# A perceiver layer on one core: the attention's value product in two passes per head, and weight sums in halves or later

## The reference, cut to what matters

```python
def _L0_xattn_ref(q, latent_kv, Wq, Wkv_expand, Wout):      # q: 512 x 1024; the mask leaves 512 keys
    qh, kh, vh = ...                                         # 16 heads of 64
    scores = where(causal, qh @ kh.T / 8, -inf)
    return concat(softmax(scores) @ vh) @ Wout.T

def _L0_attn_ref(x, w_gate, norm_gate, w_down, norm_down):   # w_gate 5632 x 1024, w_down 1024 x 2816
    def weight_quant(w):
        scale = 1.0 / clip(mean(abs(w)), 1e-5, None)
        return clip(round(w * scale), -1, 1) / scale
    gate, up = split(bitlinear(x, w_gate, norm_gate))        # bitlinear: rms norm, integers of x, w quantised
    return bitlinear(silu(gate) * up, w_down, norm_down)

x = x + _L0_xattn_ref(layernorm(x), ctx, ...)
x = x + _L0_attn_ref(layernorm(x), ...)
x = x + _L0_ffn_ref(layernorm(x), ...)                       # 8 experts, top 2, and a shared one
```

## Time and profile before

| | |
|---|---|
| time of three runs | 632.73 us median (631.98 to 633.84) |
| profiled execution | 634.08 us, its span 632.3 us, so 1.8 us lie around the span |
| TensorE | 612.3 us busy of 632.3, clock granted 0.997 |
| VectorE, ScalarE, GpSimd | 510.8, 422.5, 193.6 us busy |
| attention pairs | 34 to 147 us |
| output product | 147 to 200 us |
| gate product | 200 to 278 us |
| down product | 278 to 323 us |
| experts | 323 to 632 us |

### The profile page before, as it was taken

How to read it: one execution, slowest core, us unless ns; L and a number is a source line. 1 busy time by engine, 2 the same in 40 slices (tenths; PEclk the granted TensorE clock), 3 DMA queues, 4 the chain that set the end, 5 groups by cost and what they waited for, 6 DMA issues and landing times.

```text
span 632.3 us, 10608 instructions
## 1 busy us (share of the span) xinstructions
PE 612.3 (97%) x3624; PEld 478.2 (76%) x3625; DVE 510.8 (81%) x887; ACT 422.5 (67%) x558; POOL 193.6 (31%) x174
## 2 busy tenths in 40 slices
PE   8999999998999999999989999999999999999996
PEld 6778888887886444444557888898988989889775
DVE  5888888888787777889998569688796887969687
ACT  4998888889755989784575347557384673846630
POOL 2354446426000333527920220040431404214051
PEclk9999999999999999999989999999999999999999
DMA  8977776865246997936999467796876958779357
GB/s 333 418 294 300 304 303 238 314 262 193 101 167 265 404 374 294 384 122 251 393 368 397 195 245 280 252 369 226 318 283 240 365 222 332 262 261 354 129 171 271
DMA packets 31070, 177.91 MB, mean 281 GB/s; under 512 B 4064, under 2 KB 4064, under 8 KB 14784
## 3 DMA queue, kind: packets, MB, share of 16 engines
q1 hardware_dynamic: 25536, 158.64, 65.4%
q0 software_dynamic: 5504, 18.88, 8.2%
HBM read 154.30 MB, written 23.20 MB: 281 GB/s over the span
## 4 chain that ended last, share of the span: by engine, by line
PE 62%; DVE 15%; ACT 13%; issue 5%; DMA 3%; POOL 2%; DVEq 0%; POOLq 0%; SPq 0%; ACTq 0%
PE BK L2155 11%; PE BK L306 9%; PE BK L1884 8%; PE BK L2158 4%; ACT RA L1385 4%; ACT PR L1412 4%; PE BK L312 3%; PE BK L313 3%; PE BK L318 3%; PE BK L2125 3%; DVE WL L1033 2%; PE BK L2113 2%; PE BK L1829 2%; PE BK L2111 2%; DMA RX<-wbit 1%
## 5 line engine op out<-in xcount | busy, mean ns | idle before, releaser
L2155 PE MATMUL BK<-EX,WH 128*128 128x320 f32 x384 | 99.4, 342 | 0.0
L702 POOL TENSOR_TENSOR WL<-RC,WH 128x2048 fp32r<-128x2048 f32 x7 | 45.6, 6517 | 167.6 <-ACT WH L1588 167.6
L1033 DVE TENSOR_TENSOR WL<-RA,WH 128x2048 fp32r<-128x2048 f32 x40 | 89.4, 2287 | 9.0 <-ACT WH L1588 8.8
L2158 PE MATMUL BK<-EX,WL 128*128 128x160 f32 x336 | 79.3, 236 | 0.0
L1588 ACT ACTIVATE WH<-RA 128x2048 fp32r<-128x2048 f32 x40 | 73.6, 1904 | 0.3 <-PE BK L1927 0.2
L2155 PEld LDWEIGHTS BK<-EX,WH 128*128 128x128 f32 x384 | 69.2, 189 | 0.0
L2158 PEld LDWEIGHTS BK<-EX,WL 128*128 128x128 f32 x336 | 64.1, 191 | 0.0
L652 POOL TENSOR_TENSOR HB<-HB,ND (+2 forms) x26 | 28.7, 1122 | 100.3 <-DVE BH L919 99.7
L1484 ACT ACTIVATE RA<-RA,RT 128x2048 int16<-128x2048 f32 x22 | 43.8, 1999 | 3.0 <-DVE RT L849 2.0
L1693 ACT ACTIVATE HX<-SR 128x320 fp32r<-128x320 f32 x16 | 7.6, 472 | 57.0 <-DVE SR L1083 57.0
L1884 PE MATMUL BK<-TG,XQ 128*128 128x512 bf16 x192 | 42.4, 379 | 0.1
(11 more groups left out here) (331 smaller groups left out, 1672.6 us busy)
## 6 DMA issues: line engine op xcount, KB each, us to landing
RA<-wbit SPq DMA_DIRECT2D x54, 1024.0 KB, 6.4
RA<-wmoe SPq DMA_DIRECT2D x40, 1024.0 KB, 6.4
RC<-wmoe SPq DMA_DIRECT2D x20, 1024.0 KB, 7.9
rows<-ZERO POOLq DMA_DIRECT2D x40, 256.0 KB, 8.1
XG<-rows SPq DMA_DIRECT2D x10, 512.0 KB, 3.6
rows<-YS SPq DMA_DIRECT2D x9, 512.0 KB, 4.2
RA<-wqk SPq DMA_DIRECT2D x7, 640.0 KB, 8.1
RA<-wo SPq DMA_DIRECT2D x4, 1024.0 KB, 7.8
```

The lines of the kernel that those rows point to most:

```text
L702: e.tensor_tensor(WL[2][:, at], RC[5][:, :], WH[2][:, at].bitcast(f32), ALU.subtract).then_inc(free_c[5], 1)
L1033: e.tensor_tensor(WL[m][:, q * RAW:q * RAW + RAW], RC[j][:, :], WH[m][:, q * RAW:q * RAW + RAW].bitcast(f32), ALU.subtract)\
L2155: mm = e.matmul(bank[GBK[f]][:, 0:2 * R], WH[m][:, at], EX[:, k, :, :].rearrange("p a b -> p (a b)"), start=k == 0, stop=k == KD - 1)
L2158: e.matmul(bank[GBK[f]][:, 0:R], WL[m][:, at], EX[:, k, 0, :], start=False, stop=False)
```

## The change

Five things change together. (1) The high and low values of a head stand side by side in one stationary operand (`VS`), so `attend` needs two passes per head, one over the high weights and one over the low ones, each head into a bank of its own (2 and 7). (2) The two halves of a bank are then added: ScalarE copies the low half to SBUF (`low_values`), VectorE adds (`values_out`), ScalarE makes the high part (`out_hi`), GpSimd the low part (`out_lo`, from VectorE). The block of scores that shares bank 2 waits for the addition. (3) In each pair, ScalarE and VectorE sum one gate chunk each, in two halves (`absum_half`); the other sums leave the attention. (4) The gate's total is made alone at the old place. The sums of the 11 down chunks come later: eight on ScalarE (`late_absum`, through the buffers `DS`), three on VectorE (`absum_down`), and their total and scale in the middle of the gate product, where TensorE waits for them twice. (5) The order of the output product, of its weights' high and low parts, and of the loads changes.

TensorE:

```diff
-                e.wait_ge(s("ot_lo"), c)          # project_first
+                e.wait_ge(s("av_ev"), c * 2)
...
+                    if i == 1:                    # scores
+                        if not isinstance(c, int):
+                            e.wait_ge(s("av_ev"), c * 2 + 1)
...
+            def attend(c, banks, more):
+                e.wait_ge(s("vp_lo"), c + 1)
+                for h in range(2):
+                    if h and more:
+                        e.wait_ge(s("k_lo"), c + 2)
+                    if h and more:
+                        e.wait_ge(s("pt_hi"), c * 2 + h + 1)
+                    else:
+                        e.wait_ge(s("pt_lo"), c * 2 + h + 1)
+                    for T in (PTH, PTL):
+                        if h and more and T is PTL:
+                            e.wait_ge(s("pt_lo"), c * 2 + h + 1)
+                        for j in range(NT):
+                            m = e.matmul(bank[banks[h]][:, j * P:TOK],
+                                         VS[:, j, 2 * h:2 * h + 2, :].rearrange("p a b -> p (a b)"),
+                                         T[h][:, TOFF[j]:TOFF[j] + TOK - j * P],
+                                         start=T is PTH and j == 0, stop=T is PTL and j == NT - 1, skip_group_check=True)
+                    m.then_inc(s("av_pe"), 1)
...
             wout(0, 0, (0, 1), True, False)
+            e.wait_ge(s("av_ev"), 2 * NPAIR)
+            wout(3, 1, (0, 1), True, False)
             e.wait_ge(s("wo_p"), 1)
             wout(0, 0, (2, 3), False, False)
             transposes(NPAIR - 1)
+            wout(3, 1, (2, 3), False, False)
+            attend(NPAIR - 1, (2, 5), False)
...
             wout(0, 0, (4, 5), False, False)
+            wout(1, 0, range(6), True, False)
             e.wait_ge(s("wo_p"), 2)
...
             e.wait_ge(s("wsum"), 1)
+            e.matmul(bank[3][:, 0:1], ONEF[:, :], WS[:, 0:1], start=True, stop=True).then_inc(s("wsum_pe"), 1)
             for t in range(1, NT):
                 if t == 3:
                     e.wait_ge(s("wscale"), 1)
+                wout(t, 0, (6, 7) if t == 1 else range(KD), t > 1, True)
+                wout(t, 1, range(4, KD) if t == 3 else range(KD), t < 3, True).then_inc(s("y_tile"), 1)
                 rows_t(t - 1)
...
+                    if c == 5 and t == 0:         # gate_group
+                        waits(e, ("wsum", 2), ("h", 4 * c + 3))
+                        e.matmul(bank[6][:, 0:2], ONEF[:, :], WS[:, :], start=True, stop=True).then_inc(s("wsum_pe"), 1)
+                    if c == 5 and t == 2:
+                        e.wait_ge(s("wscale"), 2)
```

ScalarE:

```diff
                 if more:
-                    absum(1, bass.ds(c * 3 + 9, 1), c * 16 + 16)
+                    absum_half(c, 0)
                 else:
+                    wo_hi(0)
                 q_split(c)
                 if more:
-                    if isinstance(c, int):
-                        absum(4, slice(*((10, 11), (11, 12), (31, 32), (32, 33))[c - 1]), c * 16 + 16)
-                    absum(3, bass.ds(c * 3 + 11, 1), c * 16 + 16)
+                    absum_half(c, 1)
                 else:
-                    wo_hi(0)
                     wo_hi(1)
+                for h in range(2):
+                    low_values(c - 1, h)
+                values_hi(c)
                 out_hi(c - 1)
...
             exponentials(NPAIR - 1)
-            wo_hi(3)
             probs_hi(NPAIR - 1)
             e.wait_ge(s("vp_lo"), NPAIR)
             wo_hi(2)
+            for h in range(2):
+                low_values(NPAIR - 1, h, (2, 5))
+            wo_hi(3)
+            out_hi(NPAIR - 1, AO_LAST)
+            absum_kept(4, 3, 16 * 3, None)
+            absum_kept(3, 2, 16 * 3, (free_a[4], 2))
+            absum_kept(2, 1, 16 * (NPAIR + 1), (free_a[3], 2))
+            late_absum(0)
+            late_absum(1)
...
             for j in range(1, 4):
                 rounded(j, 0)
+            late_absum(2)
+            e.wait_ge(sum_x[0], 4)
             rows_out(0)
             root(e, col(2)[:, 1:2], col(3)[:, 1:2])
             rounded(0, 1)
+            late_absum(3)
             rounded(1, 1)
+            late_absum(4)
             rows_out(1)
             root(e, col(2)[:, 2:3], col(3)[:, 2:3])
+            late_absum(5)
             rounded(2, 1)
             rounded(3, 1)
+            late_absum(6)
             rows_out(2)
...
             for n in range(7):
                 head_block(n)
+                if n == 1:
+                    late_absum(7)
```

SyncE, from the wait for the first low weights of the output on (`DS[0]` lies on `XQ`, `DS[1]` on `RD`):

```diff
+        LATE = ((3, 0), (4, 1), (5, 0), (6, 1), (7, 1), (8, 1), (9, 1), (10, 1))
...
+            e.wait_ge(s("t_pe"), 2 * NPAIR)
+            late_load(0)
             e.wait_ge(s("wo_p"), 2)
             sum_load(2, 1, None)
...
             e.wait_ge(s("wo_d"), 2)
-            for n in range(4):
+            late_load(1)
+            late_free(0)
+            late_load(2)
+            bit_load(0, 4, "tern", 1)
+            late_free(1)
+            late_load(3)
+            for n in range(1, 4):
                 bit_load(n, 4 + n, "tern", 1 + n)
-            down_load(1, "raw_d")
+            for n in range(4, len(LATE)):
+                late_free(n - 1)
+                late_load(n)
             e.wait_ge(s("y_tile"), NT)
             e.dma_start(ND[:, :], n_down.partition_broadcast(P)).then_inc(s("nd_in"), 16)
-            for n in range(4):
+            for n in range(2):
                 bit_load(n, 8 + n, "tern_a", 1 + n)
             down_load(0, in_x[0])
+            late_free(len(LATE) - 1)
+            down_load(1, "raw_d")
+            for n in range(2, 4):
+                bit_load(n, 8 + n, "tern_a", 1 + n)
             down_load(2, in_x[1])
```

VectorE and GpSimd:

```diff
+            def values_out(c, to=AO, banks=(2, 7)):
+                if to is AO:
+                    e.wait_ge(s("ot_lo"), c + 1)
+                for h in range(2):
+                    e.wait_ge(s("av_b"), c * 2 + h + 1)
+                    e.tensor_tensor(to[HEADS[h], :], bank[banks[h]][HEADS[h], :], BT[HEADS[h], :], ALU.add)\
+                        .then_inc(s("av_ev"), 1)
...
                 probs_lo(c - 1)
+                if more:
+                    absum_half(c, 0)
+                else:
+                    e.wait_ge(s("q_pe"), c + 1)
+                    wo_lo(0)
                 q_split(c)
                 if more:
-                    absum(2, bass.ds(c * 3 + 10, 1), c * 16 + 16)
-                else:
-                    wo_lo(0)
-                out_lo(c - 1)
+                    absum_half(c, 1)
+                values_out(c - 1)
...
             gate_weights(5)
+            absum_down(0, in_x[0], 2)
             group(3)
+            absum_down(1, s("raw_d"), 7)
+            absum_down(2, in_x[1], 3)
+            down_total()
+            gate_weights(6)
             pair_max(0)
-            gate_weights(6)
             group(4)
+            down_scales()
...
             with e.Fori(2, NPAIR) as c:           # GpSimd
                 w_split(c)
                 v_lo(c - 1)
+                out_lo(c - 2)
...
+            out_lo(NPAIR - 2)
             wo_lo(3)
```

More of the change, by code:

```diff
@@ L33 @@
 RAW = 2048
-NABS = 2 * GC + GC
+NGS = 2 * GC + 12
+NABS = NGS + GC
 NS = 3
@@ L204, in program @@
         assert b.at == RA[1].manual_sbuf_range[0]
+        DS = [nc.alloc_sbuf_tensor_at(f"DS{j}", [P, RAW], f32, offset=T.manual_sbuf_range[0]) for j, T in enumerate((XQ, RD))]
         b.at = a.at
@@ L447, in pair_loads @@
                 qk_load(c)
-                for j in (1, 2, 3):
-                    sum_load(j, c * 3 + 8 + j, c)
-            for c in (2, 3, 4):
-                pair_loads(c)
-                sum_load(4, (11, 31, 32)[c - 2], c)
-            with e.Fori(5, NPAIR - 1) as c:
+                for j in (1, 2):
+                    sum_load(j, c * 2 + 7 + j, c)
+            pair_loads(2)
+            for m in range(2):
+                e.wait_ge(free_a[WO_SLOTS[m]], 1)
+                wo_load(m)
+            with e.Fori(3, NPAIR - 1) as c:
                 pair_loads(c)
             qk_load(NPAIR - 1)
-            e.wait_ge(free_a[4], 5)
-            wo_load(0)
-            sum_load(1, 30, NPAIR - 1)
-            e.wait_ge(free_a[3], NPAIR - 1)
-            wo_load(1)
             e.wait_ge(free_a[2], NPAIR - 1)
@@ L493, in _ @@
             e.wait_ge(s("zq"), NT)
-            down_load(3, "raw_e")
+            down_load(3, "x_in2")
             for n in range(4):
@@ L768, in absum, with absum_half @@
                     .then_inc(free_a[j], 1)
+            def absum_half(c, half):
+                if half == 0:
+                    e.wait_ge(in_a[2], c * 16 + 16)
+                ins = e.tensor_reduce(ACCW[:, bass.ds(c * 2 + 9 + 12 * half, 1)], RA[2][:, HALVES[half]], AX.X, ALU.add,
+                                      apply_absolute_value=True)
+                if half:
+                    ins.then_inc(free_a[2], 1)
             def k_split(c):
@@ L880, in _ @@
                 e.wait_ge(sum_x[j], 1)
[L881 removed]
```

(33 more changed lines are left out.)

120 lines of the change are left out of this document (62 added, 58 removed).

## The result

The changed kernel takes 652.84 us (median of 5 runs, 652.09 to 653.11) and the kernel before 633.84 (631.98 to 634.99): ratio 1.0295, interval 1.0282 to 1.0308, so 19 us slower. The forecast was 646.0, slower, with a range of 637 to 657.

The account below looks back on a forecast made before the run. ScalarE bounded pairs 1 to 4, then TensorE was full up to the down product. About 8.5 us gained in pairs, 5.2 given back; final lateness 8.4 + 4.9 = 13.3, so 632.73 + 13.3 = 646.0 us, range 637 to 657.

Parts of the forecast that it names:

- 1. The pairs: Attention: a pair falls from 15.65 to 14.4 us on TensorE, about -8.5 us; last pair starts at 122.2.
- 2. The first total: Behind the last pair: 5.2 us given back; total and matmul at 162.6 (165.89 before), TensorE waits 2.3.
- 3. Tiles 0 and 1: Output product: gate_rows(0) starts at 163.4, TensorE waits 2.7 for first integers, fourth clamp ends at 183.6.
- 4. The late sums: Before and in early gate product: load 4 lands at 192.9, VectorE stands 6.0 us, TensorE's eighth block 8.4 us late.
- the rival "faster": Late sums and second total hidden if load 4 lands within 3.0 us of the clamp: 628 us, chance 0.11.
- 5. The second total: Gate product: VectorE's three sums and later loads make TensorE wait 3.2 us, down_scales cost 1.7 more: +4.9.
- 6. The clock: New idle times at 199, 210 and 247 cost up to 1.7 us each, taken up by later waits: nothing added.
- The rule weighed: Output's last low part: VectorE excluded by GpSimd until 155.2, otherwise there at 152.2; TensorE needs it at 158.9, same sum.
- the pairs did gain: Rival of no gain in the pairs: additions of 0.9 us make VectorE the bound, 15.6 us a pair; 655 us, chance 0.05.
- the late sums did hold up the copies: Rival that only the second total costs: late sums don't hold up the roots; 633 us, chance 0.08.
- the recorded bounds: Late sums and second total: +11 if each load adds 2.4 us with 1.5 fixed, +19 if 2.8 each.

Follow-up runs that it names:

- e12_wo_late: Changed kernel with the first two output-weight loads moved behind the last query and key weight load in SP's list: 652.27 us, ratio 1.0276.
- e5_wo_hi3: Changed kernel with wo_hi(3) on ScalarE ahead of the last two low copies, not behind them: 650.63 us, ratio 1.0259.
- e1_load_early: Changed kernel with load 4 of the late sums issued ahead of the third and fourth bit loads: 648.02 us, ratio 1.0216.
- e2_four_left_out: Changed kernel without late sums 4 to 7 and their loads, constants in their columns: 635.14 us, ratio 1.0019.
- e7_root_first: Changed kernel with late_absum(4) on ScalarE behind rows_out(1) and root(2), SP's list unchanged: 651.83 us, ratio 1.03.
- e3_no_second: Changed kernel without VectorE's three sums, the second total, its matmul and both waits; down scale a constant: 649.84 us.
- e6_warm2: Changed kernel with 32 unused 256-column matmuls on TensorE just ahead of its wait for the second total: 651.89 us, ratio 1.0286.
- e10_loads: Changed kernel with six down sums back in the pairs, wo_hi(3) ahead of the last low copies, and SP's loads reordered: 629.78 us, ratio 0.9937.

## Why the prediction was right, and where its sizes were off

*1. The pairs.* Right in kind: 24 to 16 matmuls made 3.80 into 2.51 us (forecast 2.53), no engine but TensorE bounds a pair, and VectorE's additions and half sums fit (13.73 us busy a pair, 13.9 forecast). The pair takes 14.62, not 14.4: mask and scores take 2.92 in place of 2.67, where I had 0.1 for the second way of writing the mask. And the gain by the last pair is 5.5 us in place of 8.5. The term that was mis-sized is what the other order of the loads costs: I gave it nothing. It is 1.9 us (e12_wo_late), through a load that makes GpSimd late and GpSimd that makes VectorE's `normalise` long. The rest, 1.1 to 1.2, is the 0.2 a pair: e12_wo_late still starts its last pair 1.2 us after the forecast's 122.2. That this execution began late isn't in it: others that began at 34.0 to 34.2 stood at the late load instead, and had their last pair at 125.3 to 125.7.

*2. The first total.* Forecast as 40.4 us behind the start of the last pair, measured 41.1. The row of steps (`wo_hi(3)`, GpSimd 4.63, load, sum) is as told, and e5_wo_hi3 shows that it sets the place.

*3. Tiles 0 and 1.* From the start of `gate_rows(0)` to the end of the fourth clamp 20.2 us were forecast and 20.5 measured (167.33 to 187.8). At the first turning the wait was 2.8 to 3.0 us in seven of the experiments (2.7 forecast); in the changed kernel's own trace, in e1_load_early and in e2_four_left_out matmuls at the lower clock fill it.

*4. The late sums.* The step held, and carried the result. Load 4 was issued 1.3 us behind the clamp in place of 0.4, and landed after 9.6 in place of 8.9: together 1.6 late, on top of a clamp that was 4.2 late by steps 1 to 3. From its landing on, each time of the forecast is met when it is moved by 5.6 to 5.9 us: 198.79 (192.9), 205.64 (199.9), 212.63 (206.9), last copy ended 225.2 (219.6). TensorE's wait at the third block is 3.93 in place of 6 to 7: 2 us of it went to the lower clock (15 matmuls in 5.58 us; in e7_root_first 16 took 3.62), the rest to a start of the gate product at 206.09, 6.6 after the forecast's. The step's own figures give 219.6 - 211.4 = 8.2 where it writes 8.4. What I put wrongly is the weight within the step. I called VectorE's stand and the gate product's start decisive; e7_root_first takes both away and gains nothing, because load 6 and its sum still come ahead of `rows_out(2)`. My sum had this chain too (+8.4 at the eighth block), so the number didn't suffer; the rival "faster" did: it was to decide at a landing of load 4 within 3.0 us, and that alone would not have decided it.

*5. The second total.* Forecast +4.9, measured +6.7 from the last copy to `XQ` to the down product, of which e3_no_second shows 5.45 (5.2 to 7.0 with the spread) to be the total's. (Its landing "near 237.5" is 236.9 by the step's own terms, 222.2 + 0.3 + 1.9 + 5 x 2.5.) VectorE has next to no gap from 241.93 to the total at 253.93: its three sums of 2.28 us and the work it owes set the time, 4.1 us after TensorE has come. For the other 1.2 us I have no run, and the spread is as large; the loads of the gate's chunks behind the late loads are what I suspect.

*6. The clock.* TensorE ran at its lower level (1.2 GHz) for some 6 us after 2.33 us without work, again after the 7.87, and again at the second total. The forecast had no such stretch at the first total, and at most 1.7 us for each. At the first total 14 matmuls of 512 columns took 172.93 - 166.81 = 6.12 us, 2.9 more than 14 at 0.228. That all this adds nothing, since another wait lies behind each stretch, holds in two places that were tried (e6_warm2, e7_root_first).

*The rule weighed.* I took the exclusion of VectorE and GpSimd only to the last low part of the output, where both answers gave the same sum. There it came true. VectorE's timeline in the changed kernel:

```profile
154.81 4.70 DVE L886 TENSOR_TENSOR OTL<-AO_LAST,OTH 128x512 fp32r<-128x512 f32 x1 [1.03 <-ACT OTH L1500]
```

GpSimd's step ran from 154.34 to 158.97, and this row, 0.6 us of work by the forecast, ends 0.54 us after it; TensorE did not have to wait for it. But the exclusion also mattered in the pairs, in a form that I hadn't looked for (below).

*The sum.* At the down product the forecast is 7.1 us short: 5.3 of it are there at the last copy to `XQ` (3.0 from step 1, 0.7 from step 2, the rest mostly step 4's load), 1.8 come from step 5. In this execution 1.4 come back behind it, so 5.7 remain of the span. The rivals: the pairs did gain, the late sums did hold up the copies, and they weren't hidden. Up to the down product the errors all have one sign, so none hid another. That the +19 of the recorded bounds is also the measured +19.0 is luck: it was worked out for loads of 2.8 us each, and the lateness came mostly from steps 1, 2 and 5.

## What to carry to other kernels

A buffer that is loaded, summed and loaded again costs its full round (here 4.9 + 2.0 us, after the first one's 9.6) each time, and whatever stands behind the last of these sums on the same engine waits for all of them; look for the last, not for the wait that TensorE shows first. When work is taken out of a stage, check where each moved load then stands in the queue, and who waits for the load behind it: the two output weights cost 1.9 us by making the query weights late. A sum belongs where its engine has slack and where its load holds up no other: one chunk more in each of six pairs cost 0.2 us a pair in the attention (14.84 in e10_loads against 14.65 in e12_wo_late), and four chunks 20 us at the gate product.

## What the runs showed of the hardware that was not expected

VectorE's four multiplications of `normalise` (float32, SBUF to SBUF, by a scalar per row) take 1.27 us, and 3.10, 3.68 and 4.39 us beside a busy GpSimd; in the changed kernel one step took 1.42 us, where none took more than 0.49 in e12_wo_late. In the same stretch the maxima (`TENSOR_REDUCE` from PSUM) took 3.27 us as ever. The Trainium skill says as much (SBUF — State Buffer, "Who interferes with whom"): `tensor_scalar` can use the pair of ports that GpSimd shares, `tensor_reduce` on this chip never does; by that page the one that comes first keeps it for its whole instruction. The trace agrees; which of several instructions of GpSimd held it isn't resolved.

TensorE's clock doesn't follow from the length of the last idle time alone. In front of the first total's matmul TensorE had no work for 2.26, 2.39 and 2.42 us in e7_root_first, e6_warm2 and e3_no_second, and the clock in the window from 166 to 172 was 1.00. At the same place it had none for 2.33, 2.36 and 2.43 us in the changed kernel, e1_load_early and e2_four_left_out, and the clock was 0.51, 0.55 and 0.52. In all six it was 1.00 in the window from 160 to 166. The windows of the changed kernel and of e7_root_first:

```profile
166.00:172.00 6.00, 5.64 (x14) 4.55 (x15) 4.80 (x12) 5.51 (x5) 0.00 (x0) 0.51 0.72 273
```

```profile
166.00:172.00 6.00, 6.00 (x28) 5.00 (x29) 5.20 (x12) 5.51 (x6) 0.00 (x0) 1.00 0.68 249
```
